# Projection, norm and router of a decoder layer in groups of four token tiles, and the order of the first loads of cross attention

## The reference

```python
x = layernorm(x + self_attention(x))           # rotary positions, distance bias, softmax, @ proj_w.T + proj_b
x = layernorm(x + cross_attention(x, context)) # softmax, @ Wo.T
logits = x @ router_w.T                        # 8 experts, the best two of each token
x = layernorm(x + mix_of_two_experts(x))       # 256 -> 1024 -> gelu -> 256
```

## Time and profile before

| what | us |
| --- | --- |
| median of 3 runs | 2447.13 |
| the 3 runs | 2448.28, 2441.9, 2447.13 |
| span of the profiled execution, first to last instruction | 2413.0 |
| PE busy in the span | 1915.3 |
| VectorE busy | 1425.2 |
| ScalarE busy | 1166.9 |
| GpSimd busy | 303.5 |

### The profile page before, as it was taken

The page is one execution under the profiler, slowest core; times in us unless marked ns, Lnnn a source line. Parts: engine busy times, 40 slices in busy tenths (PEclk is TensorE's granted clock), DMA queues, the critical chain, the costliest instruction groups (busy, mean ns, idle before and its releaser), DMA issues.

```text
span 2413.0 us, 34121 instructions
## 1 busy us (share of the span) xinstructions
PE 1915.3 (79%) x10020; PEld 996.1 (41%) x10020; DVE 1425.2 (59%) x2550; ACT 1166.9 (48%) x2280; POOL 303.5 (13%) x532
## 2 busy tenths in 40 slices
PE   6738999999999998558888888888755688888860
PEld 2423333333333332324333333333234577777750
DVE  6328998998989991548888878788154000000016
ACT  1111777777777777113777767677710211111110
POOL 5112222322222312000000000000003100000013
PEclk9865999999999999766999999999975798889885
DMA  6420001000100100030000000100004433333332
GB/s 228 137 87 1 22 23 38 28 23 30 36 23 25 39 4 1 0 110 12 29 25 31 22 32 21 33 20 18 1 1 159 155 131 131 131 131 131 131 97 83
DMA packets 82958, 143.64 MB, mean 60 GB/s; under 512 B 11124, under 2 KB 60941, under 8 KB 80573
## 3 DMA queue, kind: packets, MB, share of 16 engines
q1 hardware_dynamic: 79498, 133.16, 16.2%
q0 software_dynamic: 3296, 8.54, 1.1%
HBM read 105.87 MB, written 35.14 MB: 58 GB/s over the span
## 4 chain that ended last, share of the span: by engine, by line
PE 58%; DVE 17%; DMA 8%; issue 7%; SPq 3%; ACT 3%; POOL 3%; DVEq 0%; POOLq 0%; ACTq 0%
PE banks L796 16%; PE banks L786 14%; PE banks L748 10%; PE banks L945 8%; DMA XS<-xsD 6%; DVE CM L1140 5%; PE banks L859 2%; PE banks L933 2%; PE banks L702 2%; ACT XT L998 2%; DVE wset L1147 2%; DVE skip L1147 2%; DVE CM L1143 1%; POOL xsD L681 1%; POOL YG L688 1%
## 5 line engine op out<-in xcount | busy, mean ns | idle before, releaser
L998 ACT ACTIVATE XT<-banks 128x512 f32<-128x512 f32 x1240 | 671.5, 600 | 367.3 <-PE banks L786 257.2
L748 PE MATMUL banks<-oper 52*128 52x512 f32 (+1 forms) x2048 | 719.6, 448 | 113.0 <-DVE CM L1140 58.2
L786 PE MATMUL banks<-oper 54*128 54x512 f32 x1856 | 692.7, 456 | 41.3 <-ACT XT L998 20.3
L1140 DVE TENSOR_REDUCE CM<-banks 128x1 f32<-128x804 f32 x512 | 486.7, 991 | 132.5 <-PE banks L748 132.4
L786 PEld LDWEIGHTS banks<-oper 54*128 54x128 f32 x1856 | 316.7, 187 | 415.2 <-ACT XT L998 250.0
L748 PEld LDWEIGHTS banks<-oper 52*128 52x128 f32 x2048 | 345.0, 197 | 341.1 <-DVE CM L1140 192.5
L998 ACT ACTIVATE late<-banks 128x512 f32<-128x512 f32 x616 | 337.5, 600 | 110.3 <-PE banks L786 93.4
L796 PE MATMUL banks<-XT,VS 128*32 128x512 f32 x2480 | 338.1, 617 | 2.6 <-ACT XT L998 1.4
L1297 DVE COPY YS<-banks 128x256 f32<-128x256 f32 x46 | 19.5, 424 | 456.7 <-PE banks L945 456.7
L1053 ACT ACTIVATE HID<-banks,b1E 128x256 f32<-128x256 f32 x184 | 77.3, 471 | 267.6 <-PE banks L933 267.6
L945 PE MATMUL banks<-W,HID 128*128 128x256 f32 x736 | 199.3, 439 | 0.0
(11 more groups left out here) (174 smaller groups left out, 1577.0 us busy)
## 6 DMA issues: line engine op xcount, KB each, us to landing
W<-in_w1T_dram SPq DMA_DIRECT2D x23, 1024.0 KB, 7.2
W<-in_w2T_dram SPq DMA_DIRECT2D x23, 1024.0 KB, 5.8
oper<-kD SPq DMA_DIRECT2D x32, 256.0 KB
oper<-kxD SPq DMA_DIRECT2D x32, 208.0 KB
xsD<-YG SPq DMA_DIRECT2D x1, 5888.0 KB, 19.1
XS<-xsD SPq DMA_DIRECT2D x23, 256.0 KB, 6.9
ysD<-YS SPq DMA_DIRECT2D x23, 256.0 KB, 6.1
qD<-parts SPq DMA_DIRECT2D x8, 512.0 KB, 2.8
```

Source lines behind the costliest of these rows:

```text
L748: mm = pe.matmul(slot[:, n * QB:n * QB + ch], QO[64 * g:64 * g + M_ROWS, c2, col:col + P], KO[64 * g:64 * g + M_ROWS, c2, k0:k0 + ch], sta ...
L786: pe.matmul(bank, KO[64 * g:64 * g + S_ROWS, c, b * P:(b + 1) * P], QO[64 * g:64 * g + S_ROWS, c, q0:q0 + QB], start=True, stop=True).then ...
L998: act.activation(PT[(c * plan.nu + u) % PRING], S[(c * plan.nu + u) % SBANKS], ACT.Exp).then_inc(A.exps, 1)
L1140: dve.tensor_reduce(CM[:, a, b:b + 1], slot.rearrange("p (n k) -> p n k", n=2)[:, :, 0:ch], AX.XY, ALU.max).then_inc(A.freed, 1)
```

## The change

`project_norm`, its copies on ScalarE and its norms on VectorE run over NG = 4 groups of GT4 = 4 tiles. A group's heads are transposed into one bank for each half of the channels and copied to `ATT` (now in the memory of `late`) 512 columns at a time; a group's products go to two banks of two tiles; VectorE adds 512 columns at a time, takes statistics tile by tile, and does the small operations on four columns at once; ScalarE scales and shifts the four tiles (Identity with a scale and a bias for each partition), which VectorE did before. The router's products of a group stand two or three groups behind. The last norm keeps its form under another name. On SP, the loads are split in `load_keys` and `load_queries`. For cross attention the first three heads' keys are issued before the stores of `PREP2`, the queries after the first four of its eight stores. Later heads load queries, then keys.

```diff
+GT4 = 4
+NG = TT // GT4
-        ATT = sb("ATT", [P, 2, CT, P])
+        ATT = late[:, :, :].rearrange("p (b k) n -> p b k n", b=2)
...
                 for h in range(RING):
-                    load(h, h)
+                    load_keys(h, h)
+                    if alibi:
+                        load_queries(h, h)
                 if alibi:
                     store_parts(PREP1[16:], 16)
+                else:
+                    store_parts(PREP2[0:4], NPREP)
+                    stored(NPREP + 4)
+                    for h in range(RING):
+                        load_queries(h, h)
+                    store_parts(PREP2[4:], NPREP + 4)
+                    stored(NPREP + len(PREP2))
                 place_shift(0, 0)
...
-            store_parts(PREP2, NPREP)
-            stored(NPREP + len(PREP2))
+            stored(NPREP)
             attention_loads(XA, CROSS, qxD, kxD)
...
+                def turn_heads(g):
+                    if g:
+                        pe.wait_ge(s_att, b0 + CT * g)
+                    for k in range(CT):
+                        for q in range(GT4):
+                            mm = pe.transpose(B[k][:, q * P:(q + 1) * P], AT[:, GT4 * g + q, k * P:(k + 1) * P], idf[:, :])
+                        mm.then_inc(s_tr, 1)
+                def project(g):
+                    pe.wait_ge(s_att, b0 + CT * (g + 1))
+                    if g:
+                        pe.wait_ge(s_pjr, (call * NG + g) * 2)
+                    for q in range(GT4):
                         for k in range(CT):
+                            mm = pe.matmul(B[2 + q // 2][:, q % 2 * C:(q % 2 + 1) * C], ATT[:, g % 2, k, q * P:(q + 1) * P],
+                                           w[:, k, :], start=(k == 0), stop=(k == CT - 1), skip_group_check=True)
+                        if q % 2:
+                            mm.then_inc(s_pj, 1)
+                def turn_stream(g):
+                    pe.wait_ge(s_xn, call * TT + GT4 * (g + 1))
+                    if g:
+                        pe.wait_ge(s_xts, b0 + CT * g)
+                    for k in range(CT):
+                        for q in range(GT4):
+                            mm = pe.transpose(B[4 + k][:, q * P:(q + 1) * P], X[:, GT4 * g + q, k * P:(k + 1) * P], idf[:, :])
+                        mm.then_inc(s_xt, 1)
+                def router(g):
+                    pe.wait_ge(s_xts, b0 + CT * (g + 1))
+                    for t in range(GT4 * g, GT4 * (g + 1)):
                         for k in range(CT):
+                            mm = pe.matmul(B[7][:, t * E:(t + 1) * E], XT[:, k, t * P:(t + 1) * P], rS[:, k, :],
+                                           start=(k == 0), stop=(k == CT - 1), skip_group_check=True)
+                    if g + 1 == NG:
+                        mm.then_inc(s_log, 1)
+                turn_heads(0)
+                for g in range(NG):
+                    if g + 1 < NG:
+                        turn_heads(g + 1)
+                    project(g)
+                    if g >= 2:
+                        turn_stream(g - 2)
+                    if call and g >= 3:
+                        router(g - 3)
+                for g in range(NG - 2, NG):
+                    turn_stream(g)
+                    if call:
+                        router(g - 1)
+                if call:
+                    router(NG - 1)
...
+                save_heads(0)
+                save_heads(1)
+                for g in range(NG):
+                    p = g % 2
+                    act.wait_ge(s_grp, call * NG + g + 1)
+                    act.activation(varG[:, p, 1, :], varG[:, p, 0, :], ACT.Sqrt).then_inc(s_gsd, 1)
+                    if g + 2 < NG:
+                        save_heads(g + 2)
+                    act.wait_ge(s_gsc, call * NG + g + 1)
+                    for q in range(GT4):
+                        act.activation(X[:, GT4 * g + q, :], X[:, GT4 * g + q, :], ACT.Identity, bias=varG[:, p, 5, q:q + 1],
+                                       scale=varG[:, p, 4, q:q + 1]).then_inc(s_xn, 1)
+                    if g >= 1:
+                        save_stream(g - 1)
+                save_stream(NG - 1)
...
+            def group_norms(call):
+                for g in range(NG):
+                    p = g % 2
+                    for h in range(2):
+                        t0 = GT4 * g + 2 * h
+                        y = X[:, t0:t0 + 2, :].rearrange("p t c -> p (t c)")
+                        dve.wait_ge(s_pj, (call * NG + g) * 2 + h + 1)
+                        dve.tensor_tensor(y, B[2 + h][:, :], y, ALU.add).then_inc(s_pjr, 1)
+                    dve.wait_ge(s_pjr, (call * NG + g + 1) * 2)
+                    for q in range(GT4):
+                        link(dve.bn_stats(statsG[:, q, :], X[:, GT4 * g + q, :]), s_ln)
+                    for q in range(GT4):
+                        link(dve.bn_aggr(aggG[:, p, q, :], statsG[:, q, :]), s_ln)
+                    dve.tensor_scalar(varG[:, p, 0, :], aggG[:, p, :, 1], EPS, None, ALU.add).then_inc(s_grp, 1)
+                    dve.wait_ge(s_gsd, call * NG + g + 1)
+                    link(dve.reciprocal(varG[:, p, 2, :], varG[:, p, 1, :]), s_ln)
...
+                    link(dve.tensor_tensor(varG[:, p, 4, :], varG[:, p, 2, :], varG[:, p, 3, :], ALU.mult), s_ln)
+                    dve.scalar_tensor_tensor(out=varG[:, p, 5, :], in0=aggG[:, p, :, 0], scalar=-1.0, in1=varG[:, p, 4, :],
+                                             op0=ALU.mult, op1=ALU.mult).then_inc(s_gsc, 1)
```

More of the change, by code:

```diff
@@ L329, in layer @@
         s_pj = sem("output_projected")
+        s_pjr = sem("output_read")
         s_ln = sem("norm_chain")
@@ L455, in load, with load_keys @@
                         sp.dma_start(q[2 * D:3 * D, :], qsrc[0, head, cols]).then_inc(ld, 16)
+                def load_keys(h, c):
+                    head = bass.ds(h * D, D)
+                    ld = A.loaded[c]
+                    for g in range(2):
+                        k = KF32[64 * g + BIAS_ROWS:64 * g + M_ROWS, c, 0:plan.nk * P]
                         sp.dma_start(k[0:2 * D, :], ksrc[0:1, head, :].to_broadcast([2, D, plan.nk * P])).then_inc(ld, 16)
@@ L844, in project_norm @@
                 pe.wait_ge(A.freed, plan.ring_before(H) + 1)
[L845 to L849, removed]
-                        for k in range(CT):
[L851 to L857, removed]
-                        for k in range(CT):
[L859 to L869, removed]
@@ L875, in _ @@
             project_norm(0, SA, SELF, wp)
-            pe.wait_ge(s_xts, TT)
-            pe.wait_ge(s_xn, TT)
+            pe.wait_ge(s_xts, NG * CT)
             prep(PREP2, NPREP)
@@ L883, in _ @@
             project_norm(1, XA, CROSS, xwo)
[L886 to L891, removed]
             pe.wait_ge(s_aux, 4)
@@ L1009, in transposes, with save_heads, save_stream @@
             def transposes(call):
[L1010 to L1024, removed]
+                b0 = call * NG * CT
+                def save_heads(g):
+                    for k in range(CT):
+                        act.wait_ge(s_tr, b0 + CT * g + k + 1)
+                        if g >= 2 and k == 0:
+                            act.wait_ge(s_pj, (call * NG + g - 1) * 2)
+                        act.activation(ATT[:, g % 2, k, :], B[k][:, :], ACT.Copy).then_inc(s_att, 1)
+                def save_stream(g):
+                    for k in range(CT):
+                        act.wait_ge(s_xt, b0 + CT * g + k + 1)
+                        act.activation(XT[:, k, GT4 * g * P:GT4 * (g + 1) * P], B[4 + k][:, :], ACT.Copy).then_inc(s_xts, 1)
+                save_heads(0)
[13 more added lines that the diff above has]
+                save_stream(NG - 1)
             attention(SA, SELF)
@@ L1057, in _ @@
             for t in range(TT):
-                root(2 * TT + t)
+                root(t)
         @block.vector
@@ L1191, in norms @@
                         b = s % 2
[L1192 to L1195, removed]
+                        y = AT[:, s, :]
                         link(dve.bn_stats(stats[:, b, :], y), s_ln)
@@ L1200, in norms @@
                         t, b = s - 1, (s - 1) % 2
-                        y = X[:, t, :] if call < 2 else AT[:, t, :]
-                        dve.wait_ge(s_sd, call * TT + t + 1)
+                        y = AT[:, t, :]
+                        dve.wait_ge(s_sd, t + 1)
                         link(dve.reciprocal(var[:, b, 2:3], var[:, b, 1:2]), s_ln)
@@ L1304, in _ @@
             dve.wait_ge(s_mix, 2 * TT)
[L1305 removed]
+            last_norms()
 def _tables():
```

30 lines of the change are left out of this document (20 added, 10 removed).

## The result

The changed kernel took 2360.93 us (median of 4 runs, 2346.13 to 2374.06) where the kernel before took 2447.7 (4 runs beside it): ratio 0.9643, interval 0.9595 to 0.969.

What follows compares the result with a forecast made beforehand. Around both projections a per-tile ring through PE and VectorE was taken as the bound. Gains of 26 (first call), 32 (second) and 6 (cross attention's start) sum to 64 us: 2447.1 to 2383, range 2362 to 2402.

Steps and rivals of the forecast that it cites:

- the grouped stage: Both projection stages in four-tile groups: 5.8 us a group at full clock, about 8.5 at half.
- Mixed as before (60% at half): Both projection stages: half clock for 60% as in the old first stage, giving 42 us in the first, 48 in the second.
- its two ends, 34 and 47.6 us: First projection stage, grouped: 34 us if wholly at full clock, 47.6 if wholly at half.
- the forecast's own mix of 36.9 and 56: Second projection stage with routers: 36.9 us at full clock, 56 at half; mixed 48, a gain of 32.
- Rival (a): Both projection stages stay at full clock: 83 us less, 2364; chance 0.12.
- rival (d): Grouped stages: Identity and the root don't share a table, two loads per group, 13 us more, 2396; chance 0.03.
- its 3.46 a group: Second projection stage: a group's 16 router product records take 3.46 us at half clock, half that at full.
- (e): Grouped stages: groups don't overlap, 20 us each at half clock, 80 a call; 20 us slower, 2467; chance 0.02.
- (f): Grouped stages: nothing to measure, groups at 15 to 16 us because they overlap only in part; chance 0.03.
- The zero fill: Fill of `xsD` after the last norm, 19.1 us to land: stays covered before the slots by some 4 us or more.
- Rival (c): Cross attention's start: fifth store not held up, 10 us more gain, 2373; or held like `kxD`, 2389; chance 0.10.
- 34.1 more, which I keep: Whole kernel: the median of the runs lies 34.1 us above the profiled span of 2413.0, and this is kept.

Runs made afterwards that it cites:

- before_filled: Kernel before plus two more 256-column products behind each tile's projection, into an unused bank: first stage 62.6 us, second 76.4 us, ratio 1.001.
- before_again: Kernel before, unchanged, profiled a second time: first stage 65.2 us, start 42.9, second stage 81.2; ratio to its other runs 0.9975.
- after_again: Changed kernel, unedited, run again beside the kernel before: first stage 34.1 us, start 38.4, second stage 42.6; 2351.01 us, ratio 0.9695.
- router_last: Changed kernel with all router products behind the last transposes: second stage 49.4 us; ratio 0.9773 to the kernel before, two runs.
- one_head_first: Changed kernel with only the first head's query loads ahead of the fifth store, the others behind the last store: start 26.9 us, ratio 0.9744 to the kernel before.
- queries_last: Changed kernel with all eight stores ahead of the twelve query loads: start 32.1 us; 2358.25 us, two runs.

## Why the prediction was wrong

Direction, places and order of the terms were right. The size was not, and the step that failed is in "the grouped stage": **"Mixed as before (60% at half)"**, used in both stages. It has two errors.

- The share. In the first stage the half clock held for a quarter of the time (0.88), not for 60%. In the old ring PE was busy for half the time, in the groups for 71%. before_filled shows in both stages that the clock goes with what PE does: with PE kept busier in the old ring it is 0.97 and 0.89, though the chain is untouched.
- The place, and this counts in both stages. The sum spreads the low clock evenly between its two ends, 34 and 47.6 us. But three turns at 8.5 instead of 5.8 make 8.1 of these 13.6 us, and the turns ran at the full clock, 5.56 us. The low clock fell where it costs less. In the second stage its share was 52% (0.74), near the 60% of the forecast, and by the forecast's own mix of 36.9 and 56 that would be 47 us: measured 43.6. In the first stage the mix would give 37: measured 34.0.

The forecast carried a stage's mean clock over, where the schedule needs the clock of each part. More on what sets the clock of a part isn't settled by these runs. Rival (a), full clock in both stages, had 0.12; it is right for the turns and the first stage's length, and wrong for the tail and the exposed routers.

That 34.0, 34.1 and 34.1 us (three profiles) match the full clock's schedule to a tenth is partly luck: three turns took 16.7 instead of 17.4, the head to the first scales 11.5 instead of 11.7, and the tail 5.8 instead of 4.9, at half clock and with slower scalings.

The terms, forecast and measured on the two first profiles:

| term | forecast | measured |
| --- | --- | --- |
| first stage | 68.1 to 42 = 26 | 68.2 to 34.0 = 34 |
| second stage | 79.9 to 48 = 32 | 79.9 to 43.6 = 36 |
| cross attention's start | 6 | 4.9 |
| sum | 64 | 75 |

Against before_again and after_again it is 31.2, 38.5 and 4.5, in all 74. The 11 us between the two sums are the failed step, 8 in the first stage and 4 in the second, less 1 at the start.

The other 11 us, to the 87 of the medians, are no part of the stages. With the stages' 75 alone the forecast would be 2373, inside its range; that the median came out 1 us below it is these 11 us. The spans of the two first profiles differ by 68.6, less than 75, for cross attention ran longer in the profile after. The line of before for it, to be set beside the three of after and before_again above:

```profile
1072.50:1746.50 674.00, 581.31 (x3596) 243.12 (x3596) 505.82 (x606) 448.77 (x848) 4.70 (x13) 0.96 0.07 23
```

The same 3596 products take 674 us at a clock of 0.96, 684 at 0.93, 691 at 0.92, 700 at 0.90, with both kernels on either side. That is 26 us from run to run in products that the change leaves alone. What makes the clock fall there in one run and not in the next isn't settled; nothing in these runs ties it to the change. The second comparison (0.9695, 2422.64 less 2351.01 = 72 us) agrees with 75; the first comparison's 87 has four runs a side and an interval that starts at 76 (3.1% of 2447.7), so 75 lies just outside it.

Step by step:

- VectorE's group: 5.8 forecast, 5.56 measured; two adds take 1.28 us, not 1.46. VectorE is the bound at the full clock, as said.
- ScalarE's four scalings: 2.08 us, above the upper bound of 1.9. It didn't matter to the turn, and stands in the tail with 0.6 more than the 1.5 forecast.
- One table load for the root and the scalings in each stage (965.57 is the only one in the first), so rival (d) fell. The key loads were issued by 974.
- Second stage: the head was at half clock, the turns at full, the exposed routers at half: 43.6 lies between the ends 36.9 and 56. That two groups of routers stand exposed was forecast right; they take 6.83 us, where the forecast puts 8.5 at half and 2.8 at full clock and doesn't say how these follow from its 3.46 a group; interleaving them is worth the 6 to 7 us of router_last.
- No root stood behind a save, no group ran in turn: (e) and (f) fell. The zero fill stayed covered: issued at 1752.17, landed 19.5 us later, at 1771.7, with the slots at 1780.0.
- The start: the fifth store waits for the queries ahead. Forecast landing 19 us after the fourth store's (1063 to 1044), measured 21 (1032.9 to 1011.8); gain 6 forecast, 4.9 measured. The forecast's own terms (1063 and 1.5 more) give 1064.5, not 1065.5, so its gain was 7. one_head_first, queries_last and the cut loads each moved it by what this mechanism gives. Rival (c) without the hold would have been 27 us, which is where the cut loads put it.
- "34.1 more, which I keep": wrong as a reading. The sum was subtracted from the median, so it didn't enter the result.

## What to carry to other kernels

Don't carry a stage's mean clock over to a new form of the stage, and don't spread it evenly. Work out head, turns and tail at both levels, and ask for each which one it will run at; here the answer was worth 11 of 75 us. A ring that passes through two engines once a tile is cut by giving each turn four tiles, and what remains is the slowest engine's own work. Before putting a load ahead of a store, look at how it is cut: loads whose slow dimension is 2 held up the stores behind them on their queue, and cutting them gave more (10.6 us at cross attention's start, 31 to 33 at self attention's) than the reordering (4.9).

## What had not been expected of the hardware

- The form of a row load: loads of 2 x 16 rows of 4 KB run at a DMA share of 0.13 and 51 GB/s when nothing else is left, and held a 512 KB store for 14.3 us; 16 rows at a time, the landing is 2.2 us and the store's 3.8.
- ScalarE takes 0.52 us for 128x256 with a scale and a bias from memory, SBUF to SBUF (2.08 for four); VectorE 0.345 apart (1.38 for four).
- Cross attention, PE busy for 86% and more, ran at a clock of 0.90 to 0.96 in four profiles of the same products, 26 us apart.
